# Layer 0 of a DLRM cross network in three products of rounded parts, with one more bank per chunk scaled by ScalarE

## What is computed

```
x0 = e                               # (512, 39, 16), gathered rows
for W in (f0, f1, f2):               # (39*39, 128), (128*39, 128), (128*39, 128)
    z  = einsum('bfd,bgd->bfgd', x0, xk).reshape(b, f*g, d)
    xk = einsum('bpd,pm->bmd', z, W) # (512, 128, 16)
result = sum over d of the three xk, side by side
```

## Time and profile before

| what | value |
|---|---|
| median of three runs | 659.31 us |
| the profiled execution's own time | 664.53 us |
| its span | 662.7 us |
| granted TensorE clock over the span | 0.995 |
| TensorE / VectorE / ScalarE / GpSimd busy | 94% / 77% / 51% / 76% |
| from one chunk's turn of x0 to the next (plain chunks) | 34.84 us |
| the same for chunks 4, 8 and 12 | 44.3 to 44.6 us |

### The profile page before, as it was taken

One profiled execution on the slowest core, in us unless ns is written; L12 is line 12 of the kernel. 1 busy time (PEld: TensorE's weight loads), 2 busy tenths in 40 slices (PEclk: granted clock), 3 DMA queues, 4 the chain that ended last, 5 costly groups with the idle time before them and its releaser, 6 DMA issues.

```text
span 662.7 us, 10828 instructions
## 1 busy us (share of the span) xinstructions
PE 620.6 (94%) x3088; PEld 467.6 (71%) x3088; DVE 512.5 (77%) x1642; ACT 338.4 (51%) x1146; POOL 502.3 (76%) x486
## 2 busy tenths in 40 slices
PE   0179999999999999999999999999999999999998
PEld 0037777777788777777788777777787777778763
DVE  4149898889886788989885788989885789989800
ACT  3015555656463555656463555656462555657602
POOL 5747989899895698889895688989895686666710
PEclk9989999999999999999999999999999999999999
DMA  6466405031311305040412304040412204000000
GB/s 217 107 162 237 131 3 131 4 88 47 88 48 39 94 3 131 3 109 26 101 34 48 85 3 132 3 120 15 104 31 59 74 4 130 0 1 2 0 1 0
DMA packets 57745, 43.38 MB, mean 65 GB/s; under 512 B 37355, under 2 KB 40683, under 8 KB 57558
## 3 DMA queue, kind: packets, MB, share of 16 engines
q1 hardware_dynamic: 51586, 37.99, 19.8%
q0 software_dynamic: 5120, 1.32, 2.6%
q10 hardware_dynamic: 980, 3.39, 1.5%
HBM read 40.74 MB, written 1.94 MB: 64 GB/s over the span
## 4 chain that ended last, share of the span: by engine, by line
PE 91%; issue 3%; another core or an unknown queue 2%; DMA 1%; ACT 1%; ACTq 1%; POOL 0%; DVE 0%; POOLq 0%; DVEq 0%
PE strip L689 22%; PE strip L690 22%; PE strip L693 21%; PE acc L650 14%; PE acc L721 4%; PE strip L707 3%; DMA g_sum<-in_L_rec_f 1%; PE strip L721 1%; PE strip L788 1%; PE acc L658 1%; ACT first L585 1%; PE strip L768 0%; PE strip L783 0%; PE strip L780 0%
## 5 line engine op out<-in xcount | busy, mean ns | idle before, releaser
L481 DVE SCALAR_TENSOR_TENSOR scaled<-strip,x_t,scaled 128x128 f32<-128x128 f32 x1216 | 332.0, 342 | 26.6 <-PE strip L693 24.1
L689 PE MATMUL strip<-w_hi,x_hi 128*128 128x512 f32 (+1 forms) x640 | 296.2, 463 | 4.1 <-ACT x_hi L530 4.1
L690 PE MATMUL strip<-w_lo,x_hi 128*128 128x512 f32 (+1 forms) x640 | 248.9, 389 | 0.0
L693 PE MATMUL strip<-w_hi,x_lo 128*128 128x512 f32 (+1 forms) x640 | 248.0, 388 | 0.0
L378 POOL TENSOR_TENSOR added<-added,product 128x512 f32<-128x512 f32 x128 | 169.7, 1326 | 80.8 <-ACT product L585 74.9
L585 ACT ACTIVATE product<-strip,x_t 128x128 f32<-128x128 f32 x512 | 146.9, 373 | 139.9 <-PE strip L693 132.7
L368 POOL DMA_INDIRECT found<-in_tables,rows x160 | 157.4, 984 | 28.2 <-issue 10.8
L689 PEld LDWEIGHTS strip<-w_hi,x_hi 128*128 128x128 f32 x640 | 121.0, 189 | 52.1 <-issue 20.1
L690 PEld LDWEIGHTS strip<-w_lo,x_hi 128*128 128x128 f32 x640 | 121.3, 190 | 43.2 <-issue 25.3
L693 PEld LDWEIGHTS strip<-w_hi,x_lo 128*128 128x128 f32 x640 | 120.7, 189 | 24.1
L650 PE MATMUL acc<-z,w 117*128 117x512 f32 x224 | 116.3, 604 | 3.2 <-ACT out L560 2.6
(11 more groups left out here) (57 smaller groups left out, 202.7 us busy)
## 6 DMA issues: line engine op xcount, KB each, us to landing
shifted<-x_fields SPq DMA_DIRECT2D x112, 234.0 KB
x_thrice<-x_fields SPq DMA_DIRECT2D x16, 234.0 KB
found<-in_tables,rows POOLq DMA_INDIRECT x160
w<-in_L_rec_f SPq DMA_DIRECT2D x1, 2496.0 KB, 11.4
g_sum<-in_L_rec_f ACTq DMA_DIRECT2D x4, 512.0 KB, 8.0
x_once<-x_fields SPq DMA_DIRECT2D x16, 78.0 KB
x_fields<-found SPq DMA_DIRECT2D x16, 72.0 KB
wt<-in_W_top SPq DMA_DIRECT2D x1, 768.0 KB
```

Source lines behind the costliest of these rows:

```text
L481: dve.scalar_tensor_tensor(into, strip[:, slot_of_strip(q) % Y_BANKS, j, :], x0_t[:, c % 2, s, f:f + 1], onto, ALU.mult, ALU.add).then_inc ...
L689: pe.matmul(into, x1_hi[:, c % 2, columns], hi, start=True, stop=False)
L690: pe.matmul(into, x1_hi[:, c % 2, columns], lo, start=False, stop=False)
L693: pe.matmul(into, x1_lo[:, c % 2, columns], hi, start=False, stop=True).then_inc(strip_ready, 1)
```

## The change

Layer 0 gets the form that layer 1 has. `w0` is split once, at the start, into `w0_hi` (ScalarE) and `w0_lo` (VectorE). Each piece of `z0` is rounded by ScalarE into `z0_hi` (`high_z0`, one slot after the product), and VectorE subtracts that from `z0` into `z0_lo` (`low_z0`, two slots after). TensorE makes three float32r products of a piece in place of one float32 product. `z0` keeps two slots, the parts have three. The matmuls of layer 0 stand one slot earlier than before (11 to 29) in plain chunks. In the last sub of each chunk ScalarE takes strips 0, 2, 4, 6 and 8 in place of 0, 3, 5 and 8, so VectorE has five of them, and GpSimd adds three `product` tiles in place of two.

```diff
-BY_ACT = ((0, 3, 5, 8),) * SUBS
+BY_ACT = ((0, 3, 5, 8),) * (SUBS - 1) + ((0, 2, 4, 6, 8),)
-Z_SLOTS = 3
+Z_SLOTS = 2
+Z_PARTS = 3
-LAYER0_AT = [12, 15, 18, 21, 24, 27, 30]
+LAYER0_AT = [11, 14, 17, 20, 23, 26, 29]
+HIGH0_LATER, LOW0_LATER = 1, 2
...
-                at_least(dve, l0_step, T0 * c + t - Z_SLOTS + 1)
+                at_least(dve, z0_hi_ready, T0 * c + t - Z_SLOTS + 1)
+                at_least(dve, z0_lo_ready, T0 * c + t - Z_SLOTS + 1)
                 dve.tensor_tensor(z0[:, (T0 * c + t) % Z_SLOTS, :], shifted[0:ROWS, t, :],
                                   x0_thrice[:, c % 2, :], ALU.mult).then_inc(z0_ready, 1)
+            def low_z0(c, t):
+                at = T0 * c + t
+                dve.wait_ge(z0_hi_ready, at + 1)
+                at_least(dve, l0_step, at - Z_PARTS + 1)
+                dve.tensor_tensor(z0_lo[:, at % Z_PARTS, :], z0[:, at % Z_SLOTS, :],
+                                  z0_hi[:, at % Z_PARTS, :].bitcast(F32), ALU.subtract).then_inc(z0_lo_ready, 1)
...
             for t in range(T0):
                 products0(0, t)
+                if t:
+                    low_z0(0, t - 1)
+            low_z0(0, T0 - 1)
...
+                        if n - LOW0_LATER in at:
+                            low_z0(c + 1, at.index(n - LOW0_LATER))
                         if n in at:
                             products0(c + 1, at.index(n))
...
+            def high_z0(c, t):
+                at = T0 * c + t
+                act.wait_ge(z0_ready, at + 1)
+                at_least(act, l0_step, at - Z_PARTS + 1)
+                act.copy(z0_hi[:, at % Z_PARTS, :], z0[:, at % Z_SLOTS, :]).then_inc(z0_hi_ready, 1)
...
+                        if n - HIGH0_LATER in at:
+                            high_z0(c + 1, at.index(n - HIGH0_LATER))
...
-                pe.wait_ge(z0_ready, T0 * c + t + 1)
+                at = T0 * c + t
+                pe.wait_ge(z0_hi_ready, at + 1)
...
-                pe.matmul(acc0[:], w0[:, t, :], z0[:, (T0 * c + t) % Z_SLOTS, :],
-                          start=(t == 0), stop=(t == T0 - 1)).then_inc(l0_step, 1)
+                hi, lo = z0_hi[:, at % Z_PARTS, :], z0_lo[:, at % Z_PARTS, :]
+                pe.matmul(acc0[:], w0_hi[:, t, :], hi, start=(t == 0), stop=False)
+                pe.matmul(acc0[:], w0_lo[:, t, :], hi, start=False, stop=False)
+                pe.wait_ge(z0_lo_ready, at + 1)
+                pe.matmul(acc0[:], w0_hi[:, t, :], lo, start=False, stop=(t == T0 - 1)).then_inc(l0_step, 1)
```

More of the change, by code:

```diff
@@ L144, in build_program @@
         mask = sb("mask", [P, TILE_B])
-        w0 = sb("w0", [ROWS, T0, MAPS])
+        w0_hi = sb("w0_hi", [ROWS, T0, MAPS], F32R)
+        w0_lo = sb("w0_lo", [ROWS, T0, MAPS], F32R)
         w1_hi = sb("w1_hi", [P, FIELDS, MAPS], F32R)
@@ L157, in build_program @@
         z0 = sb("z0", [ROWS, Z_SLOTS, N])
+        z0_hi = sb("z0_hi", [ROWS, Z_PARTS, N], F32R)
+        z0_lo = sb("z0_lo", [ROWS, Z_PARTS, N], F32R)
         x1_hi = sb("x1_hi", [MAPS, 2, N], F32R)
@@ L183, in build_program @@
         w1_raw = g_sum[:, 0:FIELDS, :]
+        w0 = product[0:ROWS, :, :, :].rearrange("p k j m -> p (k j) m")[:, 0:T0, :]
         w0_mirror = added[0:ROWS, :, :, :].rearrange("p u j m -> p (u j) m")[:, 0:T0, :]
@@ L220, in build_program @@
         w0_ready = sem("w0_ready")
+        w0_hi_ready = sem("w0_hi_ready")
+        w0_lo_ready = sem("w0_lo_ready")
         w1_hi_ready = sem("w1_hi_ready")
@@ L227, in build_program @@
         z0_ready = sem("z0_ready")
+        z0_hi_ready = sem("z0_hi_ready")
+        z0_lo_ready = sem("z0_lo_ready")
         l0_step = sem("l0_step")
@@ L492, in _ @@
             dve.wait_ge(w0_in, 32)
-            dve.tensor_tensor(w0[:], w0[:], w0_mirror, ALU.add).then_inc(w0_ready, 1)
+            dve.tensor_tensor(w0, w0, w0_mirror, ALU.add).then_inc(w0_ready, 1)
             def low_w1(i):
@@ L501, in _ @@
                 low_w1(i)
+            dve.wait_ge(w0_hi_ready, 1)
+            dve.tensor_tensor(w0_lo[:], w0, w0_hi[:].bitcast(F32), ALU.subtract).then_inc(w0_lo_ready, 1)
             for t in range(T0):
                 products0(0, t)
+                if t:
+                    low_z0(0, t - 1)
+            low_z0(0, T0 - 1)
             low_w1(W1_PIECES - 1)
@@ L587, in scale @@
                 last.then_inc(product_step, 1)
-            act.dma_start(w0[:], a["w0_upper"]).then_inc(w0_in, 16)
+            act.dma_start(w0, a["w0_upper"]).then_inc(w0_in, 16)
             act.dma_start(w0_mirror, a["w0_lower"]).then_inc(w0_in, 16)
@@ L592, in _ @@
                 act.dma_start(w1_raw[:, w1_fields(i), :], a["L0_rec_f1"][:, w1_fields(i), :]).then_inc(w1_in[i], 16)
+            act.wait_ge(w0_ready, 1)
+            act.copy(w0_hi[:], w0).then_inc(w0_hi_ready, 1)
             for i in range(W1_PIECES):
@@ L595, in _ @@
                 act.copy(w1_hi[:, w1_fields(i), :], w1_raw[:, w1_fields(i), :]).then_inc(w1_hi_ready, 1)
-            keep_x0_t(0)
+            for t in range(T0):
+                high_z0(0, t)
+                if t == 1:
+                    keep_x0_t(0)
             high_x1(0)
@@ L608, in _ @@
                     if c + 1 < CHUNKS:
+                        at = PRODUCT0_LATE_AT if closes_quarter(c) else PRODUCT0_AT
+                        if n - HIGH0_LATER in at:
+                            high_z0(c + 1, at.index(n - HIGH0_LATER))
                         if n == X1_HIGH_AT:
@@ L727, in _ @@
             turn_x0(0)
-            pe.wait_ge(w0_ready, 1)
+            pe.wait_ge(w0_hi_ready, 1)
+            pe.wait_ge(w0_lo_ready, 1)
             for t in range(T0):
```

## The result

The changed kernel takes 741.47 us (median of four runs, 739.65 to 742.22), against 659.66 us for the kernel before in the same session: a ratio of 1.1232, with a 95% interval of 1.1212 to 1.1251. It is 82 us slower. The prediction had slower as its likeliest case, but with 674 us, and its range ended at 690.

What follows compares the result with a forecast made beforehand. TensorE's own queue bounds the kernel (91% of the chain), but VectorE would come to set plain chunks. 12 x 1.5 = +18.0, chunks with layer 2 -2.1, start -1.0: 659.3 + 14.9 = 674.2 us; range 650 to 690.

Steps and rivals of the forecast that it cites:

- the moved bank: Strip bank going from VectorE to ScalarE: takes 1.04 us a chunk off VectorE and adds 1.0 to ScalarE.
- the ring of waits: Layer 0 pieces: ScalarE's high_z0 waits for VectorE, and low_z0 waits for high_z0; ScalarE's part was costed at nothing.
- TensorE saves 1.2 us a chunk: Layer 0: three float32r products take 0.69 us a piece against 0.86, saving 0.17 on each of seven pieces.
- VectorE needs 34.8 us a plain chunk without new meetings, and 33.1 without any: Plain chunks: VectorE's 31.6 us plus net 3.2 gives 34.8; without today's 1.7 us of meetings with GpSimd, 33.1.
- Seven more meetings at 0.21 us each, 1.5 us: Plain chunks: seven new subtractions each lose 0.21 us to GpSimd's additions, bringing VectorE from 34.8 to 36.3 us.
- The third rival: VectorE and GpSimd block each other at random, 0.36 us for each of fifteen operations: 704 us, chance 0.13.
- GpSimd's third addition is hidden: Plain chunks: one more 1.3 us addition makes GpSimd 32.6 us, 34.1 with meetings, hidden under VectorE's 36.3.
- ScalarE at nothing: Plain chunks: seven roundings and a bank make ScalarE 25.5 us busy; delay of `first` at slot 9 costed at nothing.
- Chunks with layer 2, -0.7 each: Chunks 4, 8 and 12: a stall of 0.5 us leaves 0.7 of the 1.2 saved, -2.1 together.
- The start, -1.0: First layer 0: between 2.4 us saved if TensorE paces it and 0.6 later if the last z0 piece does; -1.0 taken.
- TensorE waits at L696: Layer 0 in plain chunks: TensorE would wait for z_lo between slots 17 and 26, about 2.7 us a chunk.
- one of the named signs of a wrong forecast: Forecast wrong if TensorE's waits are for ScalarE's z_hi or GpSimd's x_t instead of z_lo.

Runs made afterwards that it cites:

- e1: Kernel before with three float32r products in layer 0 alone, z0 written rounded, no ScalarE rounding or subtraction, the third product reusing the rounded part: 645.96 us.
- e6: Changed kernel with the old strips, no rounding on ScalarE (VectorE writes z0 rounded and subtracts it from itself) and three z0 slots: 711.25 us.
- e3: Changed kernel with the old strips, 0, 3, 5 and 8 to ScalarE in every sub: 718.67 us.
- e7: Kernel before plus seven VectorE subtractions a chunk with two SBUF inputs, which nothing waits for: 707.38 us.
- e10: Kernel before plus seven unused VectorE subtractions a chunk, with GpSimd's additions over the fields cut to 16 columns: 656.86 us.
- e9: Changed kernel with GpSimd's additions over the fields cut to 16 columns, all waits kept: 661.25 us.
- e8: Kernel before plus seven VectorE reductions a chunk with one SBUF input, which nothing waits for: 682.42 us.
- e4: Kernel before with the new strips alone (ScalarE takes 0, 2, 4, 6 and 8 in the last sub): 669.01 us.
- e11: Changed kernel with TensorE's sums over x2_t at slot 12 in place of 9: 731.47 us.
- e12: Kernel before with three products only for the layer 0 made in chunks 4, 8 and 12, old slots and strips: 658.61 us.
- e5: Changed kernel with the old strips and layer 0 spread out: later roundings, subtractions and matmuls, three z0 slots: 714.44 us.

## Why the prediction was wrong

The runs make a sum of steps, from 660.4 us: the products -14.5 (e1, 646.0); the subtractions that TensorE waits for, with layer 0 one slot earlier, +65.3 (e6, 711.3); the roundings, with two slots of `z0` in place of three, +7.4 (e3, 718.7); the new strips +22.8 (the change, 741.5).

The forecast was 14.9 us more than before, the runs gave 82. Two steps of it failed, about equally. For the moved bank the sum took 12 x 1.04 = 12 us off VectorE and put nothing on GpSimd; measured are 22.8 us more, a miss of 35. For the rest its own terms give 12 x 2.5 - 3.1 = 27 us; e3 measured 58, a miss of 31. Of these some 20 are the meetings (12 x 1.7, from e7's 39.0 us in place of 37.3), and e3 is 11.3 us above e7, in the ring of waits that was put at nothing.

- *TensorE saves 1.2 us a chunk.* Right in kind, 0.9 to 1.1 in size (e1).
- *VectorE needs 34.8 us a plain chunk without new meetings, and 33.1 without any.* The second is right: 33.9 with seven subtractions, all strips kept and next to no additions on GpSimd (e10), 33.2 in the changed kernel (e9).
- *Seven more meetings at 0.21 us each, 1.5 us.* The mechanism was right and the size was not. e7 has 39.0 us in place of 35.8 + 1.5 = 37.3, so 3.2 us for the added meetings, in all (1.7 + 3.2) / 15 = 0.33 us each. The mean of today's eight was taken from an order in which five met nothing. In the change it is 0.36. New operations fall into other places and move the old ones: in e8, whose added operations have one SBUF input, the old products rose from 798 to 960 ns. The third rival's random meeting, 0.36 us, was the better size: it gives 34.1 + 15 x 0.36 = 39.5 us for e7's plain chunk, where 39.0 were measured. Its 704 us for the change was still 37 too low, since it put no price on the third addition either. The trace of before had the means to see that 0.21 was a lucky number: in the earlier trace rows three of eight were stretched, while GpSimd was at an addition for some 60% of the time. The rule of the Trainium skill, page "SBUF — State Buffer", section "SBUF: two separate sides", that the one blocks the other for its whole instruction, held: the trace agrees with 1.76 us, 1.08 more than alone, behind an addition that had 1.2 us to run. I had given it half its weight.
- *GpSimd's third addition is hidden.* Wrong, the largest single miss, and no rival had it as its own. The new strips that bring it cost 8.6 us alone (e4), and 22.8 beside the rest (e3 to the change). The busy time of 32.6 was under VectorE's 36.3, but what counts is not the total: the last sub's addition ends on a path to slot 9 of the next chunk, on which TensorE waited for 4.9 us already. I had the row and used it only in a rival.
- *The clock was left out.* After the stall of 3.22 us TensorE works at half its clock for 6 us; e11, which removes the stall at the sums, gives 10 us back.
- *ScalarE at nothing.* At most 7.4 us (e6): small.
- *Chunks with layer 2, -0.7 each.* e3 has 43.96 and e12 the same, -0.5. In the change itself they take 44.9 to 47.4, with the new strips.
- *The start, -1.0.* The turn of chunk 1 stands at 47.36 us after the change. The profiled execution of before had it at 51.44, but the runs that leave the start as it was have it at 45.1 to 46.3 (e4, e7, e8, e10). So the start became 1 to 2 us later, and the 5.2 us by which the profile of before lay over the median were most likely an unusual start, not a price of profiling: the profiled run of the change took 741.1.

That slower was likeliest, that VectorE fills up (38.7 of 40.1 us) and that TensorE waits at L696 came as forecast. But one of the named signs of a wrong forecast came too: of TensorE's 59.6 us of waits at these three places 39.1 were for GpSimd's `x_t` and ScalarE's `z_hi`, and in the longest plain chunks VectorE is busy only 36.5 of 44.8 us. The direction was right by VectorE's sum; the size was not. How the 15 us between e9 and e1 divide between late `z_lo` and late `z_hi` was not separated.

## What to carry to other kernels

A second engine at 91% of a stage is a bound, whatever its share of the span: work moved onto it must be weighed against the gap in that stage. Operations of VectorE with two SBUF inputs beside a busy GpSimd are priced by the full wait (half of GpSimd's instruction as often as it runs: 0.36 us worked out here, 0.33 and 0.36 measured), not by the mean of an order in which they happen to pass. A busy total under the bound hides nothing on an engine whose last result somebody awaits at a fixed slot.

## What was not expected of the hardware

- Seven subtractions of 0.68 us a chunk, 105 in all, cost 47 us beside 128x512 additions on GpSimd, and left the plain interval at the 34.8 us of before beside 128x16 ones (e7, e10). An operation issued 0.1 us behind GpSimd's addition took 1.76 us in place of 0.68.
- GpSimd's gathers were longer too: mean 984 ns an issue before, 1079 in e7, 1055 in e10, where the additions are short, and 1028 in e8, with one input. That is not the number of VectorE's operations: e9, with as many of them and short additions, has 988. Single issues take 1.24 us in place of 0.96, and those of e8 and e10 lie across a product into `z0` or an added operation; why only some do was not found.
- TensorE's clock: in e5 69 waits of up to 2.0 us left it at full speed (1.0), in the change one of 3.2 us was followed by half. But the length of a wait alone does not tell. In e3 a wait of 1.28 us, the last of several in that chunk, was followed by products 0.43 us apart, and the granted clock from 356 to 360 us is 0.65:

```profile
356.25 0.50 PE L696 MATMUL acc<-z_lo,w_hi 117*128 117x512 f32 x1 [1.28 <-DVE z_lo L455]
...
357.36 0.63 PE L734 MATMUL strip<-w_hi,x_hi 128*128 128x512 f32 x1
357.79 0.63 PE L735 MATMUL strip<-w_lo,x_hi 128*128 128x512 f32 x1
```
